# Four graph layers on one core: layer 0's attention sum moves into the block builder, and its row gather goes away

## The reference

```python
# layer 0: attention, one score per edge
e = leaky_relu(concat([h[src], h[dst], emb_rel[etype]]) @ attn_w1 @ attn_w2, 0.01)[:, 0]
ex = exp(e - segment_max(e, dst)[dst])
a = ex / segment_sum(ex, dst)[dst]
agg = segment_sum(a[:, None] * h[src], dst)
out0 = relu(where(deg > 0, agg, h) + h @ loop_weight)
# layer 1: messages of x[dst] summed at src, then relu(concat([h, aggr]) @ W_upd + b)
# layer 2: two turns of segment_sum((h * norm)[src] * w[:, None], dst) * norm
# layer 3: attention with 8 heads of 64, mean over the heads, layer norm, MLP, layer norm
```

## Time and profile before

| what | value |
|---|---|
| median of 3 runs | 5610.41 us (5601.81 to 5612.47) |
| span of the profiled execution | 5607.6 us |
| the profiled execution's own time | the page gives the span alone |
| PE busy | 2765.6 us (49%) |
| PE weight loads busy | 2175.0 us (39%) |
| DVE busy | 2436.0 us (43%) |
| ACT busy | 473.0 us (8%) |
| POOL busy | 1797.6 us (32%) |

### The profile page before, as it was taken

The page is one execution under the profiler, slowest core; times in us unless marked ns, Lnnn a source line. Parts: engine busy times, 40 slices in busy tenths (PEclk is TensorE's granted clock), DMA queues, the critical chain, the costliest instruction groups (busy, mean ns, idle before and its releaser), DMA issues.

```text
span 5607.6 us, 46533 instructions
## 1 busy us (share of the span) xinstructions
PE 2765.6 (49%) x14416; PEld 2175.0 (39%) x14458; DVE 2436.0 (43%) x4207; ACT 473.0 (8%) x909; POOL 1797.6 (32%) x1742
## 2 busy tenths in 40 slices
PE   2085022122678885989898500004770001059995
PEld 1083000000157774979733400004660001059983
DVE  4068221111677776970101500006999800035565
ACT  0000000000022331003200100001220110000000
POOL 3705777777100001000000777771000077720000
PEclk8555555555555555989999655557995555555556
DMA  3102222222236665314476121110000123102210
GB/s 109 52 1 61 58 75 62 71 62 65 85 82 140 138 144 155 109 49 160 177 269 220 44 52 49 46 48 10 0 0 23 70 80 73 49 15 66 63 35 23
DMA packets 246489, 433.22 MB, mean 77 GB/s; under 512 B 140538, under 2 KB 142311, under 8 KB 231895
## 3 DMA queue, kind: packets, MB, share of 16 engines
q10 hardware_dynamic: 126001, 172.60, 12.0%
q1 hardware_dynamic: 64102, 198.46, 10.0%
q0 software_dynamic: 56256, 60.51, 5.8%
HBM read 280.32 MB, written 150.98 MB: 77 GB/s over the span
## 4 chain that ended last, share of the span: by engine, by line
PE 35%; issue 25%; another core or an unknown queue 17%; DVE 10%; POOL 9%; DMA 2%; ACT 1%; DVEq 0%; SPq 0%; ACTq 0%; POOLq 0%
POOL ring L652 8%; PE PS L1272 7%; PE PS L1196 5%; PE PS L1096 4%; PE PS L1098 4%; PE PS L989 3%; PE PS L1029 3%; PE PS L1167 3%; PE PS L992 2%; PE PS L1175 1%; DVE s_ring L1612 1%; DVE s_ring L1613 1%; PE PS L1270 1%; PE PS L1290 1%
## 5 line engine op out<-in xcount | busy, mean ns | idle before, releaser
L652 POOL DMA_INDIRECT ring<-d_h,idx_lin x1568 | 1579.1, 1007 | 598.6 <-issue 519.4
L1272 PE MATMUL PS<-arena,s_ring 128*128 x1968 | 432.5, 414 | 198.1 <-issue 198.1
L1096 PE MATMUL PS<-qa 128*125 128x150 bf16 x1050 | 412.3, 393 | 107.0 <-DVE arena L1662 46.1
L1929 DVE TENSOR_TENSOR big<-PS,big 128x800 f32<-128x800 f32 x196 | 193.8, 989 | 619.5 <-issue 335.7
L1272 PEld LDWEIGHTS PS<-arena,s_ring 128*128 128x128 f32 x1968 | 439.8, 330 | 9.2 <-issue 1.1
L1221 PE MATMUL PS<-big 128*125 128x128 bf16 x784 | 134.0, 300 | 618.5 <-issue 449.2
L1098 PE MATMUL PS<-qa 128*125 128x150 bf16 x1050 | 401.2, 382 | 0.0
L1059 PE MATMUL PS<-s_ring,arena 81*128 81x512 bf16 x196 | 121.6, 621 | 561.0 <-issue 353.3
L1221 PEld LDWEIGHTS PS<-big 128*125 128x125 bf16 x784 | 106.9, 209 | 664.8 <-issue 456.6
L671 POOL DMA_INDIRECT d_fa<-asd,start_i x25 | 50.2, 2010 | 889.5 <-DVEq L1323 882.2
L1231 PE MATMUL PS<-big,arena 125*128 125x200 bf16 x2352 | 271.6, 272 | 118.3 <-ACT arena L900 100.9
(11 more groups left out here) (445 smaller groups left out, 4572.2 us busy)
## 6 DMA issues: line engine op xcount, KB each, us to landing
big<-d_wgt SPq DMA_DIRECT2D x50, 1562.5 KB, 7.2
d_stash<-ring SPq DMA_DIRECT2D x196, 256.0 KB
arena<-d_stash ACTq DMA_DIRECT2D x196, 256.0 KB
big<-d_cnt SPq DMA_DIRECT2D x25, 1562.5 KB, 6.5
ring<-d_h,idx_lin POOLq DMA_INDIRECT x1568
d_cnt<-big ACTq DMA_DIRECT2D x13, 1562.5 KB, 5.5
d_wgt<-big ACTq DMA_DIRECT2D x13, 1562.5 KB, 15.7
d_cnt<-arena ACTq DMA_DIRECT2D x12, 1562.5 KB, 5.4
```

Source lines behind the costliest of these rows:

```text
L652: pool.indirect_dma_start(ring[:, HALF * h + s, :], None, table, bass.IndirectOffsetOnAxis(ap=idx_lin[:, CH * i + s:CH * i + s + 1], axis= ...
L1096: nc.tensor.matmul(bank(3 * half + s // 2, NP, 2 * CW, at), lhs, hot_step(half, s, W, 2 * CW), start=(s % 2 == 0), stop=False, skip_group_ ...
L1272: mm = nc.tensor.matmul(PS[:, bass.ds(place[s] + j % SUMS * BANK, D)], marks[:, j % 2, s, :], arena[:, bass.ds(at[s], D)], start=False, st ...
L1929: v_.tensor_tensor(picked.rearrange("p (s h k) -> p s h k", s=CB, h=H), free(PS[:, 0:1], [[BANK // 2, CB], [NB, H], [1, NB]], 2 * j * BANK ...
```

## The change

Layer 0's sum over edges is done as a dense product. The builder makes three matrices a block in place of two: counts, weights and alpha. As soon as a block's alpha part is complete (all 125 sources of a block by 3125 targets), PE multiplies it with `Hn` in 25 f32 products of 125 rows, 125 columns held, 64 columns moving (`agg_products`), five of them behind each of the parts 2 to 6 of the next block; ACT takes the 64 columns out (`agg_rows`). Gone are the 784 row gathers of layer 0, their stash and reload, the 816 steps with their 408 products of ones, the step tables of layer 0, and DVE's `weights_part`. `softmax0` now stands before the builder, since the builder needs alpha: alpha goes out, POOL gathers it by window in 16 pieces, PE turns it, and DVE splits it into three bf16 terms.

A step's held operand is 128 wide (`W = P`), hots lie in pairs of steps, moving columns are 225 + 150 + 150 a step, and each part starts with one product of 512 columns of zeros. A block is stored by one DMA of 2N columns. The propagation turns run over seven groups of up to four target blocks, each in three tiles of sources, with 500 moving columns and the group's evacuation and turning behind the next group's products.

```diff
-    W = NP + 1
+    W = P
     CW = WN * NB
-    HOT = QB * (W + 4 * CW)
+    QP = QB // 2
+    HOT_LO, HOT_C = QB * W, QB * 7 * CW
...
-            pool.wait_ge(S["lin_sb"], 1)
-            pool.wait_ge(S["tab_out"], 16)
-            tiles(0, d_h0, 0, 18)
             pool.wait_ge(S["idx_ready"], 1)
...
-            tiles(0, d_h0, 18, 40)
+            pool.wait_ge(S["alpha_out"], 16)
+            for g in range(DG):
+                pool.indirect_dma_start(arow[:, g * P:(g + 1) * P], None, d_al0,
+                                        bass.IndirectOffsetOnAxis(ap=tk5_i[:, g:g + 1], axis=0)).then_inc(S["arows_in"], 16)
...
-                mm = nc.tensor.matmul(bank(7, NP, 4 * NB), free(s_bf[:, 0:1], [[HALF, NP]], h * W * HALF + s_),
+                mm = nc.tensor.matmul(bank(7, P, 4 * NB), free(s_bf[:, 0:1], [[HALF, W]], h * W * HALF + s_),
...
-                for q in range(2):
+                for q in range(3):
...
+                nc.tensor.matmul(bank(half * 3, P, BANK), zero_bf[:, 0:P], zero_bf[:], start=True, stop=False, skip_group_check=True)
                 for s in range(QB):
-                    at = s % 2 * (BANK // 2)
-                    lhs = hot_step(half, s, 0, NP)
-                    nc.tensor.matmul(bank(3 * half + s // 2, NP, 2 * CW, at), lhs, hot_step(half, s, W, 2 * CW),
-                                     start=(s % 2 == 0), stop=False, skip_group_check=True)
-                    mm = nc.tensor.matmul(bank(3 * half + s // 2, NP, 2 * CW, at + CW), lhs, hot_step(half, s, W + 2 * CW, 2 * CW),
-                                          start=False, stop=False, skip_group_check=True)
+                    at = half * 3 * BANK + s * (BANK // 2)
+                    nc.tensor.matmul(PS[:, at:at + 3 * CW], step_lo(half, s), step_c(half, s, 0, 3),
+                                     start=(s % 2 == 0 and s > 0), stop=False, skip_group_check=True)
+                    for r in range(1, 3):
+                        mm = nc.tensor.matmul(PS[:, at + CW:at + 3 * CW], step_lo(half, s), step_c(half, s, 2 * r + 1, 2),
+                                              start=False, stop=False, skip_group_check=True)
                 mm.then_inc(S["part_done"], 1)
...
+                for hi in range(first, end):
+                    mm = nc.tensor.matmul(bank(7, NP, D), wides[n % 2][0:NP, 2 * N + hi * NP:2 * N + (hi + 1) * NP], Hn[:, hi, :],
+                                          start=(hi == 0), stop=(hi == NB - 1), skip_group_check=True)
...
-                v_.tensor_tensor(hot(half, W, CW), c_iota, at_c[:, :, bass.ds(k, QB)], ALU.is_equal).then_inc(S["hot_ready"], 1)
-                v_.tensor_tensor(hot(half, 0, W), lo_iota, at_lo[:, :, bass.ds(k, QB)], ALU.is_equal)
+                v_.tensor_tensor(pairs_c(half), c_iota, pair_key[:, bass.ds(k2, QP), :, :], ALU.is_equal).then_inc(S["hot_ready"], 1)
+                v_.tensor_tensor(pairs_lo(half), lo_iota, pair_lo[:, bass.ds(k2, QP), :, :], ALU.is_equal)
...
-                v_.tensor_tensor(into, hits, at_w[:, :, :, bass.ds(k, QB)], ALU.mult).then_inc(S["one_ready"], 1)
+                for p in range(QP):
+                    last = v_.tensor_tensor(pair_c(half, p, 1, 6, 1), pair_c(half, p, 0, 6, 0), at_wa[:, :, :, bass.ds(k + 2 * p, 2)], ALU.mult)
+                last.then_inc(S["one_ready"], 1)
```

More of the change, by code:

```diff
@@ L825, in block_out @@
                 for p in range(PARTS):
-                    counts_part(i, PARTS * b + p, u, p)
+                    part_out(i, PARTS * b + p, u, p)
+                    if p == 0 and not first:
+                        agg_rows(i, b - 2)
                     if p == 2 and not first:
@@ L960, in turn_nodes @@
                 pe.wait_ge(S["ht_sb"], turn + 1)
-            def turn_rows(rows, first):
-                for u in range(R_UNITS):
-                    for g in range(PERB * u, min(PERB * u + PERB, KG)):
-                        last = nc.tensor.transpose(bank(4 + u, P, P, (g % PERB) * P), rows[:, g * P:(g + 1) * P], ident[:])
-                    last.then_inc(S["rows_tr"], 1)
-                pe.wait_ge(S["rows_sb"], first + R_UNITS)
             def zero_banks(first, n, parts=NP):
@@ new lines, in dense_block @@
+            def dense_block(i, b, first=False):
+                for p in range(PARTS):
+                    part_products(i, PARTS * b + p)
+                    if p == 1 and not first:
+                        overflow(b - 1 if i is None else 2 * i + (b - 1))
+                    if p >= 2 and not first:
+                        agg_products(i, b - 1, NB // 5 * (p - 2), NB // 5 * (p - 1))
+            pe.wait_ge(S["dense_ready"], 1)
+            pe.wait_ge(S["pos_in"], 16)
+            dense_block(None, 0, True)
@@ L1151, in _ @@
+            with pe.Fori(0, NB // 2) as i:
+                dense_block(i, 1)
+                dense_block(i, 2)
+            overflow(NB - 1)
+            agg_products(None, NB - 1, 0, NB)
+            pe.wait_ge(S["share_sb"], PARTS * NB + 2)
             turn_nodes(1)
@@ L1739, in softmax0 @@
                 q = qa[:, 0:C]
[L1740 removed]
+                b0, b1, b2 = (arena[:, j * C:(j + 1) * C] for j in range(3))
                 v.wait_ge(S["score_in"], 16)
@@ new lines, in dense_block @@
+            def dense_block(i, b, first=False):
+                for p in range(PARTS):
+                    part_hots(i, PARTS * b + p)
+                    if p == 1 and not first:
+                        overflow(i, b - 1, (b - 1) % 2)
+            dense_block(None, 0, True)
+            with v.Fori(0, NB // 2) as i:
+                dense_block(i, 1)
+                dense_block(i, 2)
+            overflow(None, NB - 1, 0)
+            v.wait_ge(S["agg_out"], NB + 1)
+            v.wait_ge(S["blk_out0"], 16 * (NB // 2 + 2))
```

580 lines of the change are left out of this document (240 added, 340 removed).

## The result

The changed kernel takes 4467.29 us (median of 4 runs, 4452.41 to 4479.30), the kernel before 5611.44 in the same comparison (4 runs): ratio 0.7966, 95% interval 0.7938 to 0.7995. The forecast was 4425 with 4355 to 4640. The profiled execution took 4452.41 us, its span is 4450.3. The page's clock line is now

A forecast was written before the change was run, and what follows sets the result against it. The prediction saw the look-up, slowed beside POOL's gathers, as the widest hole; terms of −203, −727, +67, −14, −304 and −8 took 5607.6 us to 4421.6 with 3 added, stated as 4425, range 4355 to 4640.

The forecast's parts named there:

- the gather as the look-up's brake: Look-up: steps lose time while POOL gathers; without the gather 196 steps take 1.47 us each, −727 us.
- Rival 5: Look-up: the slowness was not the gather's, 171 steps keep 8.3 us; 5590 us in all, chance 0.02.
- the histogram: Histogram: without gathers and with 128-wide loads, 96 steps at 1.55 us end at 252, before 455; −203 us.
- the stretch to the first hots: Between look-up and first hots: softmax0, 16 gathers, transposes and alpha's split move in; +67 us.
- what stood behind the builder: Behind the builder: 317 us shrink to the last block's products and last store, 13 us; −304 us.
- a turn within 135 us: Propagation turns: sign that each takes at most 135 us; the term for both turns was −8 us.
- That full clock is granted is a choice: Builder: PE works nearly without a break, so full clock was assumed, read as 0.95 or more; builder term −14 us.
- Rival 1: Builder: PE stays at half clock, a block takes 36.9 us; +370 us, 4795 in all, chance 0.11.
- Rival 2: Builder: the clock falls in every block at the 4 us overflow; +50 to +200 us, 4475 to 4620, chance 0.10.
- the 551: Builder: 25 blocks of 22 us, from parts of 2.65 and 2.4 us plus 4 at an overflow; before 565.
- rival 3: Builder: pairs run one element at a time on DVE, a part takes 4.3 us; +274 us, 4700, chance 0.03.
- Rival 4: Builder and histogram: PE's loads with a stride of 2 stay long; +183 and +28 us, 4635, chance 0.05.

The follow-up runs named there:

- the 125 columns: The changed kernel with 125 columns held in place of 128, in histogram and builder: 4463.2 us against 5576.0 for the kernel before, ratio 0.8005.
- the filler: The changed kernel with 18 products of zeros on PE behind each overflow step: 3469.4 us against 3784.0 for the kernel before, ratio 0.9164.
- the sixes: The changed kernel with hots laid out in sixes in place of pairs, PE reading at 12-byte stride: 5050.6 us, against 4445.1 for the changed kernel.

## Why the prediction was right or wrong, point by point

**Right: the gather as the look-up's brake, and its size.** −930 was forecast for histogram and look-up together and −927.6 came; the removal of the gather from the kernel before showed 875 of it by itself, with steps of 1.45 us. What the forecast did not know is that the brake depends on the chip, and that its chip was of the kind that has it was luck: on the fast chip the whole change is worth some 270 us (an estimate, above), and the forecast would have been far off. Rival 5 ("not the gather's"), at 0.02, fell on the chips that have the brake.

**Right: the histogram.** 1.55 us a step was chosen from loads of 128 columns; two steps in a row show 1.68 and 1.47, and the last hots end at 255.8 (252 forecast). That the width does it is shown by the 125 columns: 25 us more, with the last hots starting at 279.8 where the sum had 280 for the old pace.

**Right: the stretch to the first hots,** +72.7 for +67. The 16 gathers began at 696.4 and stood twice for 3.28 us where they take 0.94, while DVE did the casts and subtractions of the weight's split. The Trainium skill, "SBUF — State Buffer", section "SBUF: two separate sides", says that POOL cannot write a DMA's descriptors while a vector operation in a two-port mode, such as a copy of f32, holds the port pair that both share. The trace agrees: each of the two issues ends 0.1 us behind such a cast (701.32 and 701.21, 704.91 and 704.80), and they are 2 × 2.3 us longer than the others.

**Right: what stood behind the builder** (−306 for −304) and the turns (−7 for −8). The last block's 25 products took 8.5 us (5.6 forecast), beside the store's 10.8 (8 forecast), which is what DVE waits for. The sign "a turn within 135 us" was not met, at 141 a turn; it did not follow from the forecast's own sum either (288.9 − 8 is 140 a turn).

**Wrong: the builder, +35.7 where −14 was forecast.** The step that failed is "That full clock is granted is a choice", with 0.95 or more as its mark. The clock read 0.90. It missed that mark and also the 0.5 to 0.8 that was to tell rivals 1 and 2. Rival 2's mechanism was at work in every block with an overflow: the stand of 4.28 us there lets the clock fall for the part behind it. The filler put a price on it, 48 us, just under that rival's 50 to 200, and with the filler the builder took 553 us where the sum had said 551. So the sum of parts came out at full clock, by terms that partly cancel (below), and the choice between two clocks was the miss. The row held against rival 2, that the turns keep 0.96 over waits of 9 us, was a mean over 290 us in which one such wait hardly counts. The Trainium skill, "TensorE: Matmul & The Clock Gate", section "HAM oscillation — how this bites in real kernels", says that waits make a loop start cold each time; the trace agrees, once a block. Terms inside the 551 moved too: a step is 0.245 us and not 0.22, and part 0 took 2.75 us, not 2.4. Part 1 with the overflow took 6.2 to 6.4, as the sum's 2.4 + 4 said, and with the filler parts 2 to 4 took 2.4 to 2.6 where 2.65 was said.

**Right: pairs on DVE (rival 3 fell).** 900 elements come out at 0.54 us each, start to start (three in 1.70 with the last of 0.62), 1.67 a ns. The Trainium skill, "Vector Engine (DVE) Microarchitecture Reference", section 5.1, asks, for the doubled rate of two 16-bit sources, that the innermost dimension hold more than one element, and found that two elements in all do get it. The trace agrees for runs of two inside 900 elements.

**Rivals 4 and 1.** Rival 4 fell: the loads read 105 ns and are hidden. It priced a load at 147 ns beside the columns, all of it the load's. The run with 125 columns puts the width at 25 us in 98 steps of 8 loads, 32 ns a load; what makes up the rest, the histogram's columns 16 bytes apart perhaps, was not tried. In the builder before, 150 columns took 0.204 us (L1096 at 2129.80, L1098 at 2130.01), 0.74 columns a ns. The sixes run at this pace with 128 columns held, so there the 12 bytes between columns set it and not the load. Rival 1's clock (half) is what the sixes got, at +570 us and not +370, since the slow columns come on top.

**Layer 3 and layer 1.** Layer 3 was put at 0 and gave −17, layer 1 was in no term and gave −8. Their cause was not looked for; the gather stage of layer 3 alone takes 1063, 1074 and 1078 us in three profiles of the changed kernel.

The median came 42 us above the forecast: 32 from the table, 15 from the profiled run being the fastest of four (4452 against 4467), less 4 from rounding.

## What to carry to other kernels

Before a stage is tuned, ask what the neighbours' queues do to it: here one queue of small gathers set the pace of engines that never touched its data, and on the chips where that happens, taking it away was worth three times the rest of the change. Time the kernel before on more than one chip, since on one of them the same gathers cost next to nothing. Where an engine stands for a few microseconds in every block, put work that is due anyway into the stand; it pays once for the work and once for the clock. And lay out what PE streams so that the elements of one step lie close together, 4 bytes apart and not 12, even if a vector engine would be as happy with either.

## What the runs showed of the hardware that was not expected

- One kernel, one type of chip, two times: 3784 and 5576 to 5611 us. All of the difference that was followed lies in stages beside POOL's row gathers, as hand-overs between engines. They take 1.3 to 5.7 us in layer 0's look-up (5.7 in the kernel before, from PE's L1053, 1006.65, to DVE's L1619, 1012.38) and up to 31 us in layer 3's, where they otherwise take 0.05. Only one chip took 3784, and what sets it apart is open.
- Moving operands with 12 bytes from column to column ran at 0.74 columns a ns at 1.2 GHz, with 4 bytes at 1.19.
- PE busy for 90% of 1171 us by its records stayed at 1.2 GHz with the slow columns, while with the fast columns it read 0.90 at a lower busy share (483 us of 601).
- A load of 128 columns took 148 ns where one of 125 took 326 in the histogram's stride of 16 bytes, 105 against 152 in the builder's of 4; it mattered only in the histogram, where 100 columns follow a load, and not in the builder with 150 and more.
